# A routed convolution and a windowed attention for 16 images on one core: the projections of v one pair later

## The reference, cut to what matters

```
x = x + L0(gn(x))      # mixture of convolutions
x = x + L1(gn(x))      # windowed attention

L0: mean, std per channel -> router -> softmax twice -> top 2 of 8 experts
    shared = silu(group_norm(conv1x1(x)))
    out    = shared + rw0 * silu(group_norm(conv3x3_e0(x))) + rw1 * silu(group_norm(conv3x3_e1(x)))
L1: q, k, v = qkv_w x + qkv_b            # 8 heads of 16 channels, windows of 8 x 8 pixels
    attn = softmax(q k^T / 4 + bias)     # 64 x 64 per window and head
    out  = proj_w (attn v + dwconv7x7(v)) + proj_b
```

## Time and profile before

| | |
|---|---|
| median of 3 runs | 932.93 us (929.14 to 933.0) |
| profiled execution | 934.59 us, of which the span from first to last instruction is 932.9 us |
| mean granted TensorE clock | 0.879 of full speed |
| TensorE busy | 743.6 us, 80% of the span |
| VectorE busy | 578.1 us, 62% |
| ScalarE busy | 457.7 us, 49% |
| GpSimd busy | 197.0 us, 21% |

### The profile page before, as it was taken

One profiled execution on the slowest core, in us unless ns is written; L12 is line 12 of the kernel. 1 busy time (PEld: TensorE's weight loads), 2 busy tenths in 40 slices (PEclk: granted clock), 3 DMA queues, 4 the chain that ended last, 5 costly groups with the idle time before them and its releaser, 6 DMA issues.

```text
span 932.9 us, 18414 instructions
## 1 busy us (share of the span) xinstructions
PE 743.6 (80%) x6926; PEld 422.7 (45%) x6926; DVE 578.1 (62%) x1136; ACT 457.7 (49%) x746; POOL 197.0 (21%) x289
## 2 busy tenths in 40 slices
PE   6143768888888989888989887979797989978785
PEld 5121334454545554545454545454545456534321
DVE  4724456675767666767676757575757587632296
ACT  1204546555555564646464646464646465344422
POOL 3122123131213140403130313131313020000044
PEclk9976969797979797979888988888988989999999
DMA  9224444545464545455554545454546254586435
GB/s 353 106 71 116 139 113 146 145 128 156 144 178 136 163 148 150 150 153 165 142 170 128 173 136 173 123 173 120 177 132 177 67 176 132 161 276 217 156 157 203
DMA packets 84046, 145.29 MB, mean 156 GB/s; under 512 B 24179, under 2 KB 48886, under 8 KB 83958
## 3 DMA queue, kind: packets, MB, share of 16 engines
q1 hardware_dynamic: 58102, 100.89, 34.8%
q0 software_dynamic: 21248, 25.36, 10.9%
q10 hardware_dynamic: 4608, 17.86, 5.2%
HBM read 84.21 MB, written 51.41 MB: 145 GB/s over the span
## 4 chain that ended last, share of the span: by engine, by line
PE 41%; DMA 19%; DVE 16%; ACT 8%; issue 7%; SPq 6%; POOL 1%; POOLq 1%; ACTq 0%; DVEq 0%
PE g L1061 11%; DMA sk_d<-khl 10%; PE g L1057 5%; PE g L1079 4%; PE t L1127 4%; DMA stack<-sk_d 3%; SPq L298 3%; ACT xw L540 3%; PE s L1116 3%; PE pv L1142 3%; DMA vt<-x 3%; PE t L1241 2%; PE s L1112 2%; SPq L292 2%; PE s L1241 2%
## 5 line engine op out<-in xcount | busy, mean ns | idle before, releaser
L806 DVE BATCH_NORM_STATS2 st<-y 128x6 f32<-128x512 f32 x96 | 66.6, 694 | 147.6 <-ACT y L522 147.6
L522 ACT ACTIVATE y<-g 128x512 f32<-128x512 f32 x96 | 57.2, 596 | 167.0 <-PE g L1061 87.0
L1061 PE MATMUL g<-xsh,wsel 96*128 96x512 f32 x256 | 127.8, 627 | 14.0 <-DMA xsh<-xs 10.5
L595 ACT ACTIVATE pt<-t 128x512 f32<-128x512 f32 x128 | 76.2, 597 | 118.8 <-PE t L1127 112.2
L870 DVE TENSOR_REDUCE mx<-s 128x8 f32<-128x512 f32 x128 | 87.8, 686 | 69.6 <-PE s L1116 69.6
L1127 PE MATMUL t<-ident,less 128*128 128x128 f32 x512 | 97.6, 321 | 3.7 <-DVE less L874 3.7
L1142 PE MATMUL pv<-vp,pt 128*64 128x34 f32 x2048 | 95.2, 242 | 5.0 <-ACT pt L595 4.8
L1112 PE MATMUL s<-bias,ident 128*128 128x512 f16 x128 | 56.7, 443 | 52.9 <-DMA stack<-sk_d 52.8
L1142 PEld LDWEIGHTS pv<-vp,pt 128*64 128x64 f32 x2048 | 80.1, 154 | 31.4 <-issue 25.0
L874 DVE TENSOR_TENSOR less<-s,mx 128x512 f32<-128x512 f32 x128 | 88.5, 692 | 4.4
L1079 PE MATMUL g<-xw,w 128*128 128x512 f32 x128 | 66.7, 640 | 15.4 <-ACT y L522 11.7
(11 more groups left out here) (159 smaller groups left out, 1158.5 us busy)
## 6 DMA issues: line engine op xcount, KB each, us to landing
xsh<-xs POOLq DMA_DIRECT2D x64, 210.0 KB, 5.4
stack<-sq_d SPq DMA_DIRECT2D x96, 128.0 KB, 3.1
stack<-sk_d SPq DMA_DIRECT2D x192, 64.0 KB, 2.8
xs<-xn ACTq DMA_DIRECT2D x16, 578.0 KB, 2.9
vt<-x SPq DMA_DIRECT2D x4, 2048.0 KB, 17.7
xin<-x POOLq DMA_DIRECT2D x16, 512.0 KB, 5.8
acc_d<-xr SPq DMA_DIRECT2D x16, 512.0 KB, 5.5
sq_d<-qhl SPq DMA_DIRECT2D x16, 512.0 KB, 7.7
```

The lines of the kernel that those rows point to most:

```text
L522: act.activation(y[:, k, h * HALF:(h + 1) * HALF], g[h][:, :], ACT.Identity).then_inc(g_free[h], 1)
L595: act.activation(pt[:, p % 2].rearrange("p i w n -> p (i w n)"), tbk[p % 2][:, :], ACT.Exp).then_inc(sem["exp_done"], 1)
L806: last = v.bn_stats(st[:, 2 * k + h, :], y[:, k, h * HALF:(h + 1) * HALF])
L1061: last = mm(g[h][:, :], wsel[:, k - 1, C * dy:C * dy + C], xsh[:, k - 1, dy + 16 * h:dy + 16 * h + 16, 0:W], start=(dy == 0), stop=(dy == 1))
```

## The change

In a turn, `project_v` and `v_out` move from the sixth pair (p = 5) to the seventh (p = 6), and from ahead of `turn_outputs` and `turn_out` to the pair's end. `project_vt` and `vt_out` move from the end of the seventh pair to the front of the eighth (p = 7), on ScalarE ahead of that pair's exponential. In the eighth pair TensorE issues `project_vt`, then `turn_scores` of that pair, and the first scores of the next image only after it. On VectorE `residual` part 1 moves ahead of the eighth pair's maxima and `turn_v` moves behind `residual` part 2. `bank_uses()` follows. No instruction is added or taken away.

```diff
@@ bank_uses
-        if has1:
-            use("v", b + 1)
         if has0:
             use("ot", b, (0,))
         if has1:
+            use("v", b + 1)
             use("vt", b + 1)
@@ scalar, step
+                    if p == 7 and has1:
+                        vt_out(b + 1)
                     exponential(b, p)
...
                     if p == 5:
-                        if has1:
-                            v_out(b + 1)
                         turn_out(b, 0)
                     if p == 6 and has1:
-                        vt_out(b + 1)
+                        v_out(b + 1)
@@ vector, step
-                    if p == 6:
+                    if p == 6 and has2:
+                        residual(b + 2, 0)
+                        residual(b + 2, 1)
+                    if p == 7:
+                        if has2:
+                            residual(b + 2, 2)
                         if has1:
                             turn_v(b + 1)
-                        if has2:
-                            residual(b + 2, 0)
-                    if p == 7 and has2:
-                        residual(b + 2, 1)
-                        residual(b + 2, 2)
@@ tensor, step
-                    if has1 or p < PAIRS - 1:
-                        scores(b + (p + 1) // PAIRS, (p + 1) % PAIRS)
-                    turn_scores(b, p)
+                    if p == PAIRS - 1 and has1:
+                        project_vt(b + 1)
+                        turn_scores(b, p)
+                        scores(b + 1, 0)
+                    else:
+                        if p < PAIRS - 1:
+                            scores(b, p + 1)
+                        turn_scores(b, p)
...
                     if p == 5:
-                        if has1:
-                            project_v(b + 1)
                         turn_outputs(b, 0)
                     if p == 6 and has1:
-                        project_vt(b + 1)
+                        project_v(b + 1)
```

## The result

The changed kernel takes 1007.37 us (median of 4 runs, 1005.88 to 1012.08) against 931.42 us before (4 runs): a ratio of 1.083, 95% interval 1.079 to 1.087. The profiled execution has a span of 1005.6 us, against 932.9. The prediction, 987 us with a range of 950 to 1018 and 0.89 for slower, had the direction and holds the time. It forecast a loss of 54 us, and 73 us of span came.

The account below looks back on a forecast made before the run. TensorE was taken to wait for the stacked k in 13 turns (52.8 us), with other engines' chains pacing it after. Thirteen turns at 2.6 + 1.0 (47 us), then 5.9 and 1, made 54 us: 987 us, range 950 to 1018.

Parts of the forecast that it names:

- Step 1: ScalarE's `v_out` falls behind the SiLUs and an exponential; TensorE idles 4.4 us before `project_vt` (before: 4.02).
- Step 2: From `project_vt` to the maxima of the next image's first scores: these start 2.5 us later, partly at the lower clock.
- T: Start of VectorE's maxima of the next image's first scores: 259.21 before, forecast 261.7 in the turn read.
- the middle case: Among clock cases up to the first maxima: `project_vt` slow, the rest fast, maxima at 261.7; taken for the forecast.
- the slow one: Among clock cases up to the first maxima: `project_vt`, scores and turning all slow, maxima at 262.6.
- Step 3: From first maxima through VectorE, GpSimd and ScalarE to window copy `xw`: 12.15 us, same distance as before; `xw` 2.6 us late.
- Step 4: Second TensorE idle time, 1.75 to 4.5 us, before `convolve(., 1)`'s second half; a clock drop there costs 0 to 4.6, taken 1.0.
- (c): Rival: first scores covered, nothing else late, `v_out` deciding; 912 us, or about 852 if the clock stayed high; chance 0.06.
- the fourteenth: The turn after the thirteen, which had no DMA wait: `xw` comes 5.9 us late.
- a tail: The fifteenth turn, without SiLUs, where `project_vt` waits only for `v_out`: a loss of 1 us.

Follow-up runs that it names:

- x4b: Changed kernel with six unread matmuls of 128 columns more a turn on TensorE, between the halves of `convolve(., 1)`: 964.2 us, ratio 1.036.
- x5: Kernel before with seven matmuls of 256 columns more a turn on TensorE, at the wait for the stacked k: 930.5 us, ratio 1.000.
- x10: x9 with the seven added matmuls of x5 at the wait for the stacked k: 896.7 us, ratio 0.962.
- x1b: Changed kernel with VectorE's transpose of v ahead of the maxima of the next image's first scores: 931.4 us, ratio 0.999.
- x11: x9 with `turn_scores` of the eighth pair ahead of the next image's first scores: 915.7 us, ratio 0.981.
- x7: Changed kernel with `project_v` and `v_out` back in the sixth pair, ahead of `turn_outputs` and the SiLUs: 930.3 us, ratio 1.000.
- x2b: Kernel before with VectorE's part of the change alone (`residual` part 1 early, transpose of v behind `residual` part 2): 924.4 us, ratio 0.992.
- x9: Kernel before with only `residual` part 1 moved ahead of the eighth pair's maxima on VectorE: 919.2 us, ratio 0.985.
- x8: Changed kernel with GpSimd's two passes over v behind the next turn's load of x and its `rsqrt`: 964.0 us, ratio 1.037.
- x6: x1b with the same seven added matmuls as x5, at the wait for `vn` ahead of `project_vt`: 938.2 us, ratio 1.010.

## Why the prediction was right, and where its size was off

**Step 1** held: `project_vt` waits 4.23 us for `vn` (predicted 4.4), and `v_out` starts 6.60 us after the table load. The drain that the Trainium skill adds to a table load ("ScalarE: Activation LUTs", What ACT_TABLE_LOAD costs) is not seen: the SiLU starts 1.29 us after the load does.

**Step 2** held: T came 18.0 us after k's low half, and 17.5 was predicted for the turn that I had read. As assumed, `project_vt` ran at the lower clock (3.78 us for an estimate of 3.55); the turning and most of the scores did too, so T came 5.5 us after its start, between the 4.9 of the middle case and the 5.8 of the slow one.

**Step 3** had the right chain and was 0.8 us too long: `xw` at T + 11.33, not T + 12.15. GpSimd's cast took 1.04 us there instead of 1.90. The whole shift of `xw` was therefore smaller; measured by the short turns the steps 1 to 3 cost 1.65 us a turn, where I had 2.6. I had also taken one turn for the mean of all.

**Step 4** is the term that was mis-sized. I gave the second fall of the clock 1.0 us a turn and bounded it by 4.6, half of the busy time of the slow stretch that I knew. It costs 7.3 us in each second turn, 3.4 on average, since the stretch that follows lasts 17 us and TensorE is busy for 15.5 of them. x4b shows this term by itself: 43 us. The argument that dense matmuls behind the idle time make it short was wrong. The idle time itself was well judged for the long turns (2.60 us, forecast 1.75 or more); its upper bound of 4.5 does not follow from the rows, where only 4.4 us of the stretch were slow, which at the high clock would give 1.75 + 2.2.

The sums by term: 13 turns at 1.65 and 3.4 instead of 2.6 and 1.0, 7.2 instead of 5.9 for the fourteenth, 2.9 ahead of the first where I had nothing, and a tail that gives back 2.4 where I had a loss of 1. The first two errors have opposite signs: the steps 1 to 3 were 12 us too dear in all and step 4 was 31 too cheap. That the time lies well inside the range is in that part luck.

**The rivals.** That the first scores would be covered and all else in time (c) fell at the place that it named, ScalarE's `v_out`. Its second half, that the clock would be won, is worth a remark: by the rule of the Trainium skill ("TensorE: Matmul & The Clock Gate", HAM oscillation) the slow stretch behind the DMA wait should cost time. x5 took most of it away and won nothing; x10 did the same after VectorE's part had been shortened and won 22 us. Here the slow clock cost only where TensorE was the bound.

**What caused the loss.** Four kernels have the early `residual` part 1 and the swap, and differ in the two late pieces only (in x1b the transpose stands ahead of the first maxima, as early as a late `vn` allows):

| `v_out` | transpose of v | kernel | ratio to before |
|---|---|---|---|
| early | early | x11 | 0.981 |
| late | early | x1b | 0.999 |
| early | late | x7 | 1.000 |
| late | late | changed kernel | 1.083 |

Against the kernel before neither piece loses anything by itself, because the early `residual` part 1 pays for it. Against x11 each costs about 17 us by itself, and both together 95 (estimates from the ratios, at 931 us). Without the swap the late transpose costs 6 us (x2b against x9). So some 60 us come only when both are late: T is 3 us late, and an `xw` that can't follow sooner than 11.3 us after it delays the second half of `convolve(., 1)`. At least 43 of them are the second fall of the clock in every second turn (x4b). Why the long and the short turns alternate is only read from the trace, as told above: in the short ones an early slow stretch shortens the wait for `o`. What makes the clock fall early in one turn and late in the next was not tested, and the wait's length alone does not decide it (2.60 us did, 1.6 did not, 1.46 did once in x7).

## What to carry to other kernels

When a wait is covered by work moved from elsewhere, follow the moved work's own inputs and its readers on every engine's queue: here the projection moved ahead of a DMA wait, its copy fell behind 6.6 us of table loads, SiLUs and an exponential, and its transpose ahead of a chain that another engine needed. Ask of each idle time of TensorE what runs behind it: in this kernel one of 2.6 us in front of a stretch where TensorE was the bound cost 7.3 us by the clock, and one of 4 us in front of a stretch that another engine set cost nothing by it, even at half the clock. Here it paid to shorten the other engine first and then to fill the gap (x9, x10); the filling alone showed no gain (x5). And compare a part of a change with a kernel that has all the rest of it: against the kernel before, a loss and a gain in one run look like nothing.

## What the runs showed of the hardware

The turns fell into a cycle of two lengths, 47.5 and 54.9 us, that repeated to within 0.1 us over twelve turns, with the clock's falls at the same places each time. In one slow stretch the clock stayed low for 17 us though TensorE was busy for 15.5 of them, while the stretch around the wait for `vn` lasted 6.8 us.

GpSimd and VectorE get in each other's way. The cast over v took 1.9 us in 14 turns before, where it started while VectorE's `residual` part 0 ran, and 1.04 in the changed kernel, where VectorE's reductions ran beside it (VectorE before, beside the earlier trace rows):

```profile
255.10 1.19 DVE L836 TENSOR_TENSOR xr<-y,xin 128x1024 f32<-128x1024 f32 x1
```

And while GpSimd's subtraction ran from 328.29 to 330.42, a VectorE operation on one column, which takes 0.16 us elsewhere, took 1.40 and ended with it:

```profile
329.03 1.40 DVE L795 TENSOR_TENSOR sq<-gs 128x1 f32<-128x1 f32 x1
```

x8 moved GpSimd's passes away and left VectorE's order as it is, and there the same operation is short again:

```profile
367.65 0.16 DVE L795 TENSOR_TENSOR sq<-gs 128x1 f32<-128x1 f32 x1
```

It took 1.39 to 1.41 us in 14 of 16 cases in the changed kernel and 0.16 in all 16 in x8; `residual` part 2 in x6 is another case (2.56 us for 1.27). It fits what the Trainium skill ("SBUF — State Buffer", SBUF: two separate sides) says of the port pair that the two engines share, which whoever starts first holds for a whole instruction; the one-column operation has two inputs in SBUF, as that rule asks.
